# Attention heads with key tiles in batches of 2, 2 and 3, seven exponential buffers, and head sums added in place by GpSimd

## What is computed

```
q = einsum('btd,hrd->bhtr', x, Q)          # 8 heads, r = 32
k = einsum('bud,hrd->bhur', x, K)
attn = softmax(einsum('bhtr,bhur->bhtu', q, k) / sqrt(64))
ctx = einsum('bhtu,bud->bhtd', attn, x)
out = einsum('bhtd,hde->bte', ctx, VO)     # summed over the heads
h = h + out
```

## Time and profile before

| | us |
|---|---|
| median of 3 runs | 663.7 |
| the three runs | 658.11, 664.76, 663.7 |
| the profiled execution | 657.45 |
| its span, first to last instruction | 655.6 |
| TensorE busy | 589.2 (90%) |
| VectorE busy | 401.8 (61%) |
| ScalarE busy | 338.0 (52%) |
| GpSimd busy | 70.4 (11%) |

### The profile page before, as it was taken

How to read it: one execution, slowest core, us unless ns; L and a number is a source line. 1 busy time by engine, 2 the same in 40 slices (tenths; PEclk the granted TensorE clock), 3 DMA queues, 4 the chain that set the end, 5 groups by cost and what they waited for, 6 DMA issues and landing times.

```text
span 655.6 us, 10594 instructions
## 1 busy us (share of the span) xinstructions
PE 589.2 (90%) x3080; PEld 332.6 (51%) x3080; DVE 401.8 (61%) x996; ACT 338.0 (52%) x710; POOL 70.4 (11%) x80
## 2 busy tenths in 40 slices
PE   0695988998999999999999999999999999997993
PEld 0451444553445565565665665665565565452441
DVE  3846475125687767766766766775775777245661
ACT  0466775664645545544644554554554555545511
POOL 0000000000893000000000000000000000012000
PEclk9998899998999999999999999999999999997998
DMA  7500000000632222322322322322322320000014
GB/s 159 212 0 1 0 1 0 1 0 13 154 97 73 73 68 73 77 58 74 82 54 71 89 54 70 90 54 69 85 61 60 84 70 18 2 1 0 1 43 105
DMA packets 21987, 37.65 MB, mean 57 GB/s; under 512 B 5561, under 2 KB 15225, under 8 KB 21705
## 3 DMA queue, kind: packets, MB, share of 16 engines
q1 hardware_dynamic: 21816, 37.12, 22.1%
q10 hardware_dynamic: 144, 0.20, 0.2%
HBM read 6.07 MB, written 2.41 MB: 13 GB/s over the span
## 4 chain that ended last, share of the span: by engine, by line
PE 79%; DVE 7%; ACT 4%; issue 3%; DMA 3%; POOL 2%; SPq 1%; ACTq 0%; DVEq 0%; POOLq 0%
PE P L681 76%; DMA X<-x 2%; DVE mx L1379 2%; POOL acc L667 2%; PE P L697 2%; ACT PT L585 1%; ACT L482 1%; DVE part L1420 1%; DVE xhat L1205 1%; ACT g L622 1%; DVE xs L1274 1%; PE P L1080 0%; SPq L371 0%; PE P L937 0%; DVE gate_s L1262 0%
## 5 line engine op out<-in xcount | busy, mean ns | idle before, releaser
L585 ACT ACTIVATE PT<-P 112x392 f32<-112x392 f32 x448 | 188.5, 497 | 167.7 <-PE P L681 166.6
L1379 DVE TENSOR_REDUCE mx<-P 112x1 f32<-112x392 f32 x448 | 232.8, 558 | 54.9 <-PE P L681 53.4
L681 PE MATMUL P<-PT,XVs 112*64 112x392 f32 x896 | 175.5, 507 | 0.0
L681 PE MATMUL P<-Ks,Qs 96*112 96x392 f32 x448 | 164.8, 372 | 2.5 <-DVE mx L1379 1.8
L681 PE MATMUL P<-Qs,Ks 98*112 98x392 f32 x448 | 153.6, 348 | 9.0 <-ACT PT L585 9.0
L681 PEld LDWEIGHTS P<-Ks,Qs 96*112 96x112 f32 x448 | 77.4, 175 | 91.9 <-issue 60.9
L681 PEld LDWEIGHTS P<-Qs,Ks 98*112 98x112 f32 x448 | 78.3, 176 | 19.3 <-ACT PT L585 14.1
L681 PEld LDWEIGHTS P<-PT,XVs 112*64 112x64 f32 x896 | 53.0, 136 | 61.8 <-issue 43.1
L1406 DVE RECIPROCAL zi<-P 98x1 f32<-98x1 f32 x32 | 5.4, 169 | 75.9 <-PE P L681 75.9
L681 PE MATMUL P<-VBs,CT 128*98 128x130 f32 (+1 forms) x320 | 37.2, 263 | 0.6 <-ACT CT L593 0.6
L681 PEld LDWEIGHTS P<-VBs,CT 128*98 128x98 f32 x320 | 36.4, 165 | 2.3 <-ACT CT L593 1.3
(11 more groups left out here) (183 smaller groups left out, 545.5 us busy)
## 6 DMA issues: line engine op xcount, KB each, us to landing
Qs<-QKH SPq DMA_DIRECT2D x64, 98.0 KB, 2.2
Ks<-QKH SPq DMA_DIRECT2D x64, 98.0 KB, 2.1
XVs<-XV SPq DMA_DIRECT2D x32, 196.0 KB, 2.5
Qs<-QKL SPq DMA_DIRECT2D x32, 98.0 KB, 2.1
Ks<-QKL SPq DMA_DIRECT2D x32, 98.0 KB, 2.1
X<-x SPq DMA_DIRECT2D x4, 588.0 KB
out<-OT SPq DMA_DIRECT2D x24, 98.0 KB
wa<-table_a SPq DMA_DIRECT2D x1, 2207.5 KB, 8.5
```

The source lines that it names most:

```text
L585: nc.scalar.activation(PT[:, u % PTS, c * HALF:(c + 1) * HALF], P[0:T, SCORE_BANK + half_in_loop(s, u, c) % RING, 0:HALF], ACT.Exp, scale= ...
L681: return nc.tensor.matmul(dst, lhsT, rhs, start=start, stop=stop, **more)
L1379: nc.vector.tensor_reduce(mx[:, s % 2, c, t:t + 1], bank(n)[0:T, :], AX.X, ALU.max)\
```

## The change

1. **Batches.** `BATCHES` becomes `((0, 1), (2, 3), (4, 5, 6))`. The context tiles of the last batch, 4, 5 and 6, now stand together behind batch (0, 1) of the next head.
2. **Outputs.** `head_out` of the head before is issued inside the last batch, between tile 5 and tile 6.
3. **Buffers.** `PT` has seven buffers, one per key tile. `exp_half` waits for the same tile of the head before.
4. **Sums.** GpSimd adds each head in place to `OUT[:, b, :]`: a copy for head 0 of an image, an addition for the others, 31 instructions in a row without a loop. `acc`, `group_out` on ScalarE, `image_sum` on VectorE and the addition at L1464 are gone; `OUT` has four slots in place of eight. VectorE adds only the very last head.
5. **Waits.** `divide_block` waits on GpSimd's counter `added` where it waited on `sums`; the final transposes wait on `added` for images 0 to 2.

```diff
-BATCHES = ((0, 1), (2, 3), (4, 5), (6,))
+BATCHES = ((0, 1), (2, 3), (4, 5, 6))
-PTS = 4
+PTS = 7
...
-                    scalar.wait_ge(av_done, NT * n + (u - 3 if u >= 4 else u - 6 if u == 3 else u - 2))
+                    last = u - PTS if u >= PTS else u + (NT - 1 - u) // PTS * PTS - NT
+                    scalar.wait_ge(av_done, NT * n + last + 1)
...
-                        if q == 3 and s == 0 and not first:
-                            group_out(i - 1)
-            def group_out(i):
-                scalar.wait_ge(sums, 3 * i + 3)
-                nc.scalar.activation(OUT[:, i, :], acc[:, 0, :], ACT.Copy).then_inc(grouped, 1)
...
+            def add_head(b, h):
+                pool.wait_ge(proj_done, HEADS * b + h + 1)
+                if h == 0:
+                    nc.gpsimd.tensor_copy(OUT[:, b, :], part[:, 0, :]).then_inc(added, 1)
+                else:
+                    pool.wait_ge(added, HEADS * b + h)
+                    nc.gpsimd.tensor_tensor(OUT[:, b, :], OUT[:, b, :], part[:, h % HG % 3, :], ALU.add).then_inc(added, 1)
+            for n in range(NH - 1):
+                add_head(n // HEADS, n % HEADS)
...
                         for u in tiles:
+                            if u == NT - 1 and not (first and s == 0):
+                                used = ...
+                                head_out(i if s else i - 1, (s - 1) % 4, first and s == 1, block_bank(s), used)
...
-                        if q == 2 and not (first and s == 0):
-                            used = ...
-                            head_out(i if s else i - 1, (s - 1) % 4, first and s == 1, block_bank(s), used)
...
                 if s == 3:
-                    vector.wait_ge(sums, 3 * i + 1)
+                    vector.wait_ge(added, 4 * i + 1)
                 elif s == 0 and not first:
-                    vector.wait_ge(sums, 3 * i)
+                    vector.wait_ge(added, 4 * i)
...
-                        if u == 5 and s < B - 1 and final:
-                            image_sum(s)
...
-            nc.vector.tensor_tensor(OUT[:, 2 * B - 1, :], OUT[:, 2 * B - 2, :], acc[:, 1, :], ALU.add).then_inc(vec_step, steps.one())
```

More of the change, by code:

```diff
@@ L175, in build @@
         part = sb(reg2, "part", [GT, 3, NQ * D])
-        acc = sb(reg2, "acc", [GT, 2, NQ * D])
-        OUT = sb(reg2, "OUT", [GT, 2 * B, NQ * D])
+        OUT = sb(reg2, "OUT", [GT, B, NQ * D])
         sb(reg2, "past_norm", [128, 160])
@@ L258, in build @@
         proj_full, proj_done, block_done = sem("proj_full"), sem("proj_done"), sem("block_done")
-        sums, grouped, summed, join_full = sem("sums"), sem("grouped"), sem("summed"), sem("join_full")
+        added, summed, join_full = sem("added"), sem("summed"), sem("join_full")
         stored = [sem(f"stored{b}") for b in range(B)]
@@ L987, in four_heads @@
                         for u in tiles:
+                            if u == NT - 1 and not (first and s == 0):
+                                used = (HEAD_HALVES * (4 * ahead[0] + ahead[1]) + 2 * (NT - 1) - RING + 1) if more else HEAD_HALVES * NH
+                                head_out(i if s else i - 1, (s - 1) % 4, first and s == 1, block_bank(s), used)
                             for c in range(2):
@@ L999, in four_heads @@
                             max_turn(i + (s == 3), (s + 1) % 4)
-                        if q == 2 and not (first and s == 0):
-                            used = (HEAD_HALVES * (4 * ahead[0] + ahead[1]) + 2 * (NT - 1) - RING + 1) if more else HEAD_HALVES * NH
-                            head_out(i if s else i - 1, (s - 1) % 4, first and s == 1, block_bank(s), used)
                         if q > 0:
@@ L1032, in _ @@
             for b in range(B):
-                pe.wait_ge(summed, b + 1)
+                if b < B - 1:
+                    pe.wait_ge(added, HEADS * (b + 1))
+                else:
+                    pe.wait_ge(summed, 1)
                 for k in range(NGT):
                     for h in range(2):
-                        last = mm(P[h * D:(h + 1) * D, 2 + b, k * GT:(k + 1) * GT], OUT[:, 2 * b, (2 * k + h) * D:(2 * k + h + 1) * D],
+                        last = mm(P[h * D:(h + 1) * D, 2 + b, k * GT:(k + 1) * GT], OUT[:, b, (2 * k + h) * D:(2 * k + h + 1) * D],
                                   Bt("ident", GT)[:, 0:GT])
@@ L1421, in divide @@
                                         zi[:, 0:NQ - 1].unsqueeze(2).broadcast_to([GT, NQ - 1, D]), ALU.mult).then_inc(proj_done, 1)
-            def image_sum(b):
-                vector.wait_ge(grouped, 2 * b + 2)
-                nc.vector.tensor_tensor(OUT[:, 2 * b, :], OUT[:, 2 * b, :], OUT[:, 2 * b + 1, :], ALU.add).then_inc(summed, 1)
             def four_heads(i, first=False, final=False):
@@ L1461, in _ @@
             four_heads(7, final=True)
-            vector.wait_ge(grouped, 2 * B - 1)
-            vector.wait_ge(sums, 3 * (2 * B - 1) + 2)
-            nc.vector.tensor_tensor(OUT[:, 2 * B - 1, :], OUT[:, 2 * B - 2, :], acc[:, 1, :], ALU.add).then_inc(vec_step, steps.one())
             divide_block(7, 3, block_bank(0), None)
@@ L1468, in _ @@
             vector.wait_ge(proj_done, NH)
-            nc.vector.tensor_tensor(OUT[:, 2 * B - 2, :], OUT[:, 2 * B - 1, :], part[:, 0, :], ALU.add).then_inc(summed, 1)
+            vector.wait_ge(added, NH - 1)
+            nc.vector.tensor_tensor(OUT[:, B - 1, :], OUT[:, B - 1, :], part[:, 0, :], ALU.add).then_inc(summed, 1)
             for b in range(B):
```

## The result

| | before | changed |
|---|---|---|
| median, first session | 660.9 (657.43 to 664.76, 4 runs) | 638.57 (637.66 to 640.51, 4 runs) |
| ratio, 95% interval | | 0.9665 (0.9593 to 0.9736) |
| median, second session | 661.58 (657.0 to 666.87, 17 runs) | 641.96 (640.28 to 645.64, 6 runs) |
| ratio, 95% interval | | 0.9734 (0.9699 to 0.977) |
| profiled execution, span | 657.45, 655.6 | 640.51, 638.7 |

The kernel is faster by 2.7 to 3.4%, about 20 us. The direction was right; the time was forecast at 647.5 with 639.5 as its lower end, and 638.57 lies 0.9 under it.

What follows compares the result with a forecast made beforehand. The prediction took TensorE, busy for 90% of the span, as the bound. Savings of 9.1 us (group sum) and 7.1 us (context runs) made 16.2 us, from a median of 663.7 to 647.5 us, range 639.5 to 656.5.

Steps and rivals of the forecast that it cites:

- Part A: ScalarE's group sum: removing seven copies and their waits for GpSimd saves TensorE 1.30 us each, 9.1 us in all.
- rival 2: Additions or exponentials still stop TensorE once a group, so only the batch saving stays: 656.6 us, chance 0.06.
- Part B: Context matmuls on TensorE: three runs per head instead of four save 0.23 us per head, 7.1 us over 31 heads.
- the left edge: Entry to tile 6's score matmuls: with head_out in front instead of context, its extra 0.08 us per head goes.
- the upper bound: Batch saving per head at most 0.32 us, if head_out had its own edge towards context inside its 1.08.
- the step from `head_out` to scores: On TensorE, both over more than 64 columns, so by the tiling-mode rule this step would be free.
- What has to stay hidden: VectorE's chain from tile 6 to the next head's fourth maxima keeps its 0.14 us margin; GpSimd's extra work costs zero.
- Rival 1: VectorE's chain becomes the pace, so only the gain from removing ScalarE's group sum stays: 654.6 us, chance 0.09.
- GpSimd's hold on VectorE: Shared port lock: a running GpSimd addition lengthens VectorE's small maximum from 0.16 to 0.46 us; zero on the path.
- Head 0: No head_out there, so six halves come without a pause: at most 1.4 us once, taken as zero.
- The sum on the trace: Both savings, 9.1 + 7.1 = 16.2 us, taken from the profiled execution's 657.45, giving 641.2 us.
- The carry to the median: Moved the forecast from the profiled execution to the median of runs shown, 663.7, giving 647.5 us.

Runs made afterwards that it cites:

- sums_only: Kernel before with GpSimd adding sums in place, but its batches, four buffers and output place kept; 653.13 us, ratio 0.9866 to the kernel before.
- stall_back: Changed kernel with ScalarE's wait for GpSimd's addition and a 98x512 copy put back once a group; 651.3 us.
- copy_alone: Changed kernel with ScalarE's 98x512 copy put back once a group, of a result added a head earlier; 644.91 us.
- after: The changed kernel's profiled execution in the first session, no further edit; 640.51 us.
- again: Changed kernel run once more without any edit, in the second session; 641.96 us.
- out_behind: Changed kernel with head_out issued behind context tile 6 instead of in front of it, VectorE's division waiting directly; 658.88 us.

## Why the prediction was right and where it was wrong

**Part A, right.** 9.1 us forecast; `sums_only` gave 9.3, of which 8.8 at the seven copies, and `stall_back` 7.8. The mechanism is the one stated: `copy_alone` shows that the wait is all of it. The wait didn't move, so rival 2 is out.

**Part B, right in kind, too small.** 7.1 us forecast from 0.23 per head, 9.1 measured from 0.29. The 0.15 for the run of three tiles was measured as 0.16. The step that failed is "so the left edge, 0.17 - 0.09 = 0.08, goes". That edge stayed: the first matmul behind `head_out` still takes 0.41 us and its successor comes 0.26 later. What went was an edge that I had put into the upper bound only, that of `head_out` towards context: 0.13 of its 1.08. The free edge was misread from the earlier trace rows: the two matmuls behind the seven transposes take 0.61 us there, which is 0.27 from the first start to the second and 0.34 for the second. A usual step of 0.18 would give 0.52. So the row that was read as "nothing visible at the edge" shows the edge. Nor is it tied to a change between 64 columns and the full width, from which the prediction took that the step from `head_out` to scores would be free: that step is 0.26. The prediction's bound of 9.9 held.

**What has to stay hidden, right.** The chain on VectorE keeps its margin, 0.14 us before and 0.12 now:

```profile
340.59 1.18 DVE L1374 TENSOR_REDUCE mx<-P 112x1 f32<-112x392 f32 x2
...
341.89 0.36 PE L673 MATMUL P<-Ks,Qs 96*112 96x392 f32 x1
```

The two reductions end at 340.59 + 1.18 = 341.77. TensorE waits for maxima in the first head only (0.2 us from 187 us on in `after`, 1.2 in `again`), as before. The reason given for the margin was off: tile 6's first matmul takes 0.41, not 0.34. `out_behind` shows how thin that is: with the outputs one step later the same chain costs 0.26 per head in the next batch alone. Rival 1 is out here and would have been true there. GpSimd's hold on VectorE costs nothing at 2.3 us per head; its copy of 98x512, taken at 1.29 us, takes 0.61. Head 0 cost nothing: from its first `max_turn` to the first `CT` copy it is 20.9 us before and 20.8 in `again`, both without a stretch at the lower level.

**The sum on the trace, 16.2 forecast, 18.4 measured on the heads.** The profiled execution was forecast at 641.2 and measured at 640.51. That agreement is partly luck. The changed kernel's profiled execution had a stretch at the lower level, 1.2 GHz, in its first head:

```profile
188.00:194.00 6.00, 5.94 (x17) 2.67 (x17) 3.73 (x9) 2.46 (x6) 5.73 (x8) 0.53 0.27 80
```

A run of two context tiles there takes 2.88 us instead of 1.54. From the first `max_turn` (179.3) to the first `CT` copy (202.4) it needs 23.1 us, 2.2 more than the 20.9 of the kernel before; `sums_only`, with the old batches, has the same 23.1, and `again`, the changed kernel itself, has not. So the new batches don't bring it. Whether the kernel before has it in some of its executions can't be told from its one trace.

**The carry to the median, wrong.** "Carried to the median it is 647.5 us" is the step that put the number too high. It took 663.7, the middle one of three runs, as the level of all later runs, while the trace stood at 657.45. A fourth run of the same kernel brought its median to 660.9. Of the 8.9 us between 647.5 and 638.57, 2.8 are that, 2.2 are the heads, and the remaining 3.9 are, by what is left, the part in front of the heads. It was short in the one of the four executions that was traced (first rise of the clock at 45.0, where all later traces have 61 to 64); the other three are 1.6 to 2.9 us faster still, with the same program, so theirs was short too, by estimate. That is luck of the session and not the change. In the second job, with 17 and 6 runs, the difference of the medians is 19.6. The lower end of the range had the same fault: 639.5 did not take the low level together with the upper bounds of A and B, 657.45 - 19.6 = 637.9, which was written down and would have held the result.

## What to carry to other kernels

In an in-order queue a copy that is free by its work can cost by its wait: ask which instruction stands behind it, and try the copy without the wait before removing work. Where TensorE is full, look at the starts of its matmuls, not at their durations: one more run of 64-column matmuls cost 0.32 us per head here (0.15 at its end, 0.17 at the edges of the scores around it), so fewer and longer runs pay, as long as something independent (here `head_out`) stands where another engine has to be fed early. And when the total spreads by 1% from causes outside the change, forecast and compare the stage itself, between two fixed instructions of the trace. Check a printed clock of 1.00 against the pace of equal matmuls before you rule the clock out.

## What the runs showed of the hardware

- TensorE starts this program at its lower level and first rises to the upper one at 45.0 and 45.1 us in two traced executions and at 61.2 to 64.1 in eight others. Four matmuls take 1.97 us at 46.61 in `out_behind`, at the lower level, and 1.08 at 45.59 in the kernel before, at the upper. The trace has no clock record in front of the first rise, and the views print 1.00 there. The slow stretch in the first head of the changed kernel is recorded, as 0.53.
- GpSimd's addition of 98x512 holds VectorE's small operations between SBUF buffers until it ends (0.72 instead of 0.16 us), also one with a single tensor input, and leaves reductions from PSUM alone (0.55).
- `head_out`, full-width float32, costs 0.95 us in front of full-width scores and 1.08 in front of 64-column matmuls. The first step between two scores is 0.26 to 0.27 us instead of 0.18 behind context, behind `head_out` and behind the transposes of the earlier trace rows alike.
